# Perceiver block on one core: ScalarE takes the square roots of the first norms, GpSimd loads the small parameters, and some steps of the expert routing change places

## The reference

```python
x = x + xattn(layernorm(x), ctx_1024, ...)   # [c, c2q, c*c2q, c*q2c] @ W_l.T + b_l
x = x + attn(layernorm(x), ...)              # attention, conv of width 3, attention with the new q, out_w
h = layernorm(x)
probs = softmax(h @ gate_w.T); top2_p, top2_i = top_k(probs, 2)
hh = gelu(einsum('nd,edf->nef', h, w1) + b1)
all_out = einsum('nef,efd->ned', hh, w2) + b2
x = x + clip(h + w0 * all_out[n, i0] + w1 * all_out[n, i1], -100, 100)
```

## Time and profile before

| | us |
|---|---|
| median of 3 runs | 432.95 (432.45 to 433.37) |
| the profiled execution, its own time | 431.55 |
| its span, first to last instruction | 429.9 |
| TensorE busy | 409.6 (95%) |
| VectorE busy | 332.9 (77%) |
| ScalarE busy | 212.9 (50%) |
| GpSimd busy | 60.3 (14%) |

### The profile page before, as it was taken

How to read it: one execution, slowest core, us unless ns; L and a number is a source line. 1 busy time by engine, 2 the same in 40 slices (tenths; PEclk the granted TensorE clock), 3 DMA queues, 4 the chain that set the end, 5 groups by cost and what they waited for, 6 DMA issues and landing times.

```text
span 429.9 us, 8272 instructions
## 1 busy us (share of the span) xinstructions
PE 409.6 (95%) x3090; PEld 312.9 (73%) x3090; DVE 332.9 (77%) x618; ACT 212.9 (50%) x369; POOL 60.3 (14%) x80
## 2 busy tenths in 40 slices
PE   1999999999999999999999989999999999999995
PEld 1566565688898899995568745788777778777783
DVE  4758788866259883448977999898998899899666
ACT  4345325130556343131536233796877888778510
POOL 2130000000422120112103701000000000000162
PEclk9999999999999999999999999999999999999998
DMA  7999799999960460009324659889999999995662
GB/s 254 392 379 369 237 401 375 353 408 408 409 236 23 103 247 2 2 3 367 124 93 159 235 208 381 297 324 369 383 387 350 375 382 360 392 368 198 222 193 98
DMA packets 50734, 116.74 MB, mean 272 GB/s; under 512 B 3286, under 2 KB 3302, under 8 KB 50704
## 3 DMA queue, kind: packets, MB, share of 16 engines
q1 hardware_dynamic: 38176, 92.28, 58.3%
q10 hardware_dynamic: 10448, 19.15, 11.6%
q0 software_dynamic: 2080, 4.90, 3.5%
HBM read 94.04 MB, written 21.23 MB: 268 GB/s over the span
## 4 chain that ended last, share of the span: by engine, by line
PE 67%; DMA 13%; DVE 9%; POOL 3%; ACT 3%; issue 3%; SPq 1%; ACTq 0%; DVEq 0%; POOLq 0%
PE banks L2015 4%; PE banks L2013 4%; PE banks L2014 4%; PE banks L2046 4%; DMA w<-in_wlT 3%; PE banks L1734 3%; PE banks L2057 3%; PE banks L2056 3%; PE banks L1623 3%; PE banks L2055 3%; DMA A<-in_ctxT 3%; PE banks L1744 3%; PE banks L1739 3%; PE banks L1624 3%; PE banks L1858 3%
## 5 line engine op out<-in xcount | busy, mean ns | idle before, releaser
L1374 DVE TENSOR_TENSOR w_lo<-w,w_hi 128x1024 fp32r<-128x1024 f32 x48 | 55.5, 1218 | 0.0
L662 ACT ACTIVATE w_hi<-w 128x1024 fp32r<-128x1024 f32 x48 | 47.4, 1094 | 2.1 <-DMA w<-in_w 2.1
L747 ACT ACTIVATE A<-banks,b_sb 128x128 f32<-128x128 f32 x112 | 30.4, 382 | 24.3 <-PE banks L2026 9.3
L2013 PE MATMUL banks<-w_hi,cT_r 128*128 128x512 f32 x100 | 40.1, 401 | 0.0
L2015 PE MATMUL banks<-w_hi,cT_r 128*128 128x512 f32 x100 | 39.0, 390 | 0.0
L2014 PE MATMUL banks<-w_lo,cT_r 128*128 128x512 f32 x100 | 39.0, 390 | 0.0
L858 POOL TENSOR_TENSOR A<-A,hrec 128x1024 f32<-128x1024 f32 x8 | 16.4, 2048 | 66.6 <-DVE hrec L1192 66.6
L900 POOL DMA_DIRECT2D b_sb<-in_b1T x12 | 6.5, 542 | 137.1 <-ACT A L747 121.8
L1623 PE MATMUL banks<-w_lo,A2r 128*128 128x512 f32 x52 | 22.7, 437 | 1.6 <-ACT A2r L529 1.3
L1183 DVE TENSOR_REDUCE hmax<-banks 128x16 f32<-128x1024 f32 x8 | 9.8, 1221 | 18.2 <-PE banks L1809 18.2
L2015 PEld LDWEIGHTS banks<-w_hi,cT_r 128*128 128x128 f32 x100 | 18.8, 188 | 4.0
(11 more groups left out here) (353 smaller groups left out, 1045.0 us busy)
## 6 DMA issues: line engine op xcount, KB each, us to landing
w<-in_w SPq DMA_DIRECT2D x24, 2048.0 KB, 10.3
rows_dram<-A ACTq DMA_DIRECT2D x1, 14592.0 KB, 45.6
A<-in_ctxT SPq DMA_DIRECT2D x8, 1024.0 KB, 11.0
A<-in_ctx SPq DMA_DIRECT2D x8, 1024.0 KB, 9.5
w<-in_w SPq DMA_DIRECT2D x5, 1024.0 KB, 7.6
w<-in_wlT SPq DMA_DIRECT2D x3, 1024.0 KB, 15.0
wqkv<-in_wqkvT SPq DMA_DIRECT2D x1, 3072.0 KB, 16.2
w<-in_convT SPq DMA_DIRECT2D x1, 3072.0 KB, 18.1
```

The costliest lines, as they stand in the source:

```text
L662: nc.scalar.activation(w1_hi[:, u, k * F:(k + 1) * F], w1[:, u, k * F:(k + 1) * F], ACT.Copy).then_inc(hi_ready, 1)
L747: ins = nc.scalar.activation(hT[:, u, f, :], HT[f // 4][:, tile(f % 4)], ACT.Gelu, bias=b1_sb[:, u, f:f + 1])
L1374: nc.vector.tensor_tensor(w1_lo[:, u, part], w1[:, u, part], w1_hi[:, u, part].bitcast(F32), ALU.subtract).then_inc(lo_ready, 1)
L2013: mm(HP[u][c][:, :], xr[:, 0, u, k, :], high[:, at], start=(i == 0), stop=False)
```

## The change

Four things are changed.

1. The beginning. The roots of the four variances are taken by ScalarE (`first_roots`, `other_roots`) instead of Newton steps on VectorE; a first Sqrt on `eps` brings the table in early, and an Exp behind the second brings back the table for the scores. ScalarE rounds both first halves of W_l, then takes the first high part straight from PSUM (`high_first`) and copies `cT` after it.
2. The six small parameters are loaded by GpSimd's queue: `wcq` and `wq` ahead of its first memset, `wc` and the three scalars behind its constants.
3. The routing. VectorE does `place(0)` before `finish(3)` instead of after `norm_by_root(3)`. On TensorE `turn_gate(1)` goes behind `outputs(7)` and now waits for `take_out(7)`; the first half of `out_project(3)` goes ahead of `gate_logits(1)`; `gate_logits(3)` goes ahead of `counts(2)`. `outputs(7)` no longer waits for the copy of the second turned tile.
4. The experts. ScalarE makes the gelu of block 1 before it waits for the store of block 0, and in `output(0)` TensorE turns block 2's rows after seven steps of f instead of four. The scratch `bm`, `bv` of `list_blocks` moves to other columns.

```diff
@@ scalar: beginning
-            for dst, src in ((wcq, "wcqT"), (wq, "wqT")):
-                act.dma_start(dst[:, :], t[src]).then_inc(widths_in, 16)
-            act.dma_start(wc[:, :], t["wcT"]).then_inc(score_params_in, 16)
-            for i, name in enumerate(("b_cq", "b_c", "b_q")):
-                act.dma_start(scal[:, i:i + 1], t[name].to_broadcast([P, 1])).then_inc(score_params_in, 16)
+            first_roots()
             high_wl(0)
+            high_wl(1)
+            high_first()
             copy_cT(0, 0)
-            high_part(0, 0)
-            high_wl(1)
             widen_first()
+            other_roots()
@@ scalar: first experts
+            gelu(1, 1, 16, True)
             store_first(0, 0)
-            gelu(1, 1, 16, True)
@@ gpsimd
+            for dst, src in ((wcq, "wcqT"), (wq, "wqT")):
+                pool.dma_start(dst[:, :], t[src]).then_inc(widths_in, 16)
...
+            pool.dma_start(wc[:, :], t["wcT"]).then_inc(score_params_in, 16)
+            for i, name in enumerate(("b_cq", "b_c", "b_q")):
+                pool.dma_start(scal[:, i:i + 1], t[name].to_broadcast([P, 1])).then_inc(score_params_in, 16)
@@ vector: beginning
-            dve.wait_ge(x_in[0], 16)
-            norm(0)
+            variance_first()
+            dve.wait_ge(root_ready, 1)
+            link(nc.vector.reciprocal(rstd[:, 0:1], sd[:, 0:1]))
+            normalise(0)
...
             low_wl(0)
+            low_wl(1)
+            dve.wait_ge(cT_ready, 1)
             low_part(0, 0)
-            low_wl(1)
-            norm_others()
+            variance_others()
+            dve.wait_ge(root_ready, 2)
+            link(nc.vector.reciprocal(rstd[:, 1:NT], sd[:, 1:NT]))
@@ vector: routing
             norm_by_root(2)
             after_choice(1)
+            place(0)
             finish(3)
             variance(3)
             take_counts(1)
             norm_by_root(3)
-            place(0)
@@ tensor: outputs, turn_gate
                 if m >= 2 * NT - 2:
-                    pe.wait_ge(cT_ready, m + 3)
+                    pe.wait_ge(cT_ready, 2 * NT + 1)
...
-                pe.wait_ge(o_ready, 2 * (NT + min(n + 2, NT)))
+                pe.wait_ge(o_ready, 2 * (NT + min(2 * n + 2, NT)))
@@ tensor: routing
             values(7)
-            turn_gate(1)
             counts(0)
             outputs(7)
+            turn_gate(1)
+            out_project(3, 0)
             gate_logits(1)
-            out_project(3, 0)
             out_project(3, 1)
@@
             dispatch(0, 1)
+            gate_logits(3)
             counts(2)
-            gate_logits(3)
@@ tensor: output
-                        if between and f == FT // 2:
+                        if between and f == FT - 1:
                             between()
```

More of the change, by code:

```diff
@@ L210, in perceiver_kernel @@
         slots_c = A2[:, 4096:4096 + 2 * (NT - 1) * E].rearrange("p (c t e) -> p c t e", c=2, t=NT - 1)
-        bm, bv = (A2[:, at:at + OVER * E * MORE].rearrange("p (o i) -> p o i", o=OVER) for at in (4096, 4608))
+        bm, bv = (A2[:, at:at + OVER * E * MORE].rearrange("p (o i) -> p o i", o=OVER) for at in (6144, 6656))
         cnt = c2q[:, 3 * P:3 * P + NT * 2 * E].rearrange("p (t e) -> p t e", t=NT)
@@ L515, in high_wl, with high_first, first_roots, other_roots @@
                 nc.scalar.activation(wl_hi[:, wl_half(i), :], wl[:, wl_half(i), :], ACT.Copy).then_inc(wl_high, 1)
+            def high_first():
+                act.wait_ge(cT_psum, 1)
+                nc.scalar.activation(pieces(0, 0)[:, 0], turn_bank(0, 0)[:, :].rearrange("p (k n) -> p k n", k=KT),
+                                     ACT.Copy).then_inc(part_high[0], 1)
+            def first_roots():
+                act.wait_ge(var_ready, 1)
+                nc.scalar.activation(steps[:, 0:1], eps[:, 0:1], ACT.Sqrt)
+                act.wait_ge(var_ready, 2)
+                nc.scalar.activation(sd[:, 0:1], mv[:, 0, 1:2], ACT.Sqrt, bias=eps[:, 0:1]).then_inc(root_ready, 1)
+            def other_roots():
+                act.wait_ge(var_ready, 3)
+                nc.scalar.activation(sd[:, 1:NT], mv[:, 1:NT, 1], ACT.Sqrt, bias=eps[:, 0:1]).then_inc(root_ready, 1)
+                nc.scalar.activation(steps[:, 1:2], eps[:, 0:1], ACT.Exp)
             def high_part(part, n):
@@ L709, in root @@
             def root(n):
-                act.wait_ge(var_ready, n)
+                act.wait_ge(var_ready, 3 + n)
                 nc.scalar.activation(sd[:, n:n + 1], mv[:, n, 1:2], ACT.Sqrt, bias=eps[:, 0:1]) \
@@ L932, in norm_by_root @@
             def norm_by_root(n):
-                dve.wait_ge(root_ready, n)
+                dve.wait_ge(root_ready, 2 + n)
                 link(nc.vector.reciprocal(rstd[:, n:n + 1], sd[:, n:n + 1]))
@@ L956, in norm, with variance_first, variance_others @@
                                         ALU.subtract, ALU.mult).then_inc(normed, 1)
-            def norm_others():
-                rest = slice(1, NT)
-                var, r, h = mv[:, rest, 1], rstd[:, rest], sd[:, rest]
+            def variance_first():
+                nc.vector.memset(eps[:, :], EPS).then_inc(var_ready, 1)
+                dve.wait_ge(x_in[0], 16)
+                link(nc.vector.bn_stats(st[:, 0, :], x_res[:, 0, :]))
+                nc.vector.bn_aggr(mv[:, 0, :], st[:, 0, :]).then_inc(var_ready, 1)
+            def variance_others():
                 for n in range(1, NT):
@@ L965, in norm_others @@
                     link(nc.vector.bn_stats(st[:, n, :], x_res[:, n, :]))
[L966 to L975, removed]
+                    ins = nc.vector.bn_aggr(mv[:, n, :], st[:, n, :])
+                    if n < NT - 1:
+                        link(ins)
+                ins.then_inc(var_ready, 1)
             def normalise(n):
@@ L1170, in _ @@
             link(nc.vector.memset(zero_bf[:, :], 0.0))
-            link(nc.vector.memset(eps[:, :], EPS))
             low_c(NT - 2)
```

## The result

| | before | after |
|---|---|---|
| median of the executions (us) | 432.55 (20 runs) | 435.49 (20 runs) |
| ratio of the times | | 1.0075, 95% interval 1.0059 to 1.0090 |
| span of the profiled execution | 429.9 | 433.1 |

One of the 20 executions before took 468.87 us and is left out of the ratio. By the ratio the change costs 3.2 us (2.6 to 3.9); the two medians differ by 2.9. Forecast was +1.45, with +2.65 as the upper end of the range. The direction was right, the size wrong. The median itself, 435.49, lies just inside the recorded range of 432.3 to 435.6, but only because that range was laid around a median of three executions (432.95), which twenty put at 432.55.

What follows compares the result with a forecast made beforehand. TensorE bounds the long stretches; elsewhere a start transfer, routing hand-offs and two tied VectorE and TensorE chains. -0.5 + 1.65 + 0.3 = +1.45 us on 431.55 gives 433.0, plus 1.40 to the median 434.4; range 432.3 to 435.6.

Steps and rivals of the forecast that it cites:

- the start: Up to the first scores: `scores(0)` at about 15.0 instead of 15.56, -0.5 us, between 0 and -0.75.
- the routing: From tile 1's logits to VectorE's take of block 0's rows: +1.65 us, between +0.7 and +2.2.
- Between the ends I go by the packets: Start: packet counts put the small transfers nearer to cheap in GpSimd's queue, so `ctxT` lands 0.8 us earlier.
- the start gives nothing: Rival, chance 0.15: small transfers cost the same in GpSimd's queue, `ctxT` lands at 15.4; 434.9 us.
- the filled hole: Start, TensorE: the 0.33 us wait for the third pair of weights goes; last product ends near 14.8, not 15.2.
- the turning: Routing: `turn_gate(1)` behind `outputs(7)` makes tile 1's logits 2.9 us later; +1.15 us after VectorE's slack.
- the swap: Routing: `gate_logits(3)` ahead of `counts(2)` delays VectorE's taking of the counts by another 0.5 us.
- If a step or two run side by side: Routing: the condition for the lower bound of +0.7 us instead of +1.65.
- Net +0.3 us: First expert blocks: VectorE's gapless chain 0.35 to 0.4 later, TensorE sooner but waiting; between -0.1 and +0.5.
- Smaller routing loss: Rival, chance 0.26: overlap cuts the routing to +0.7, start gives -0.7; sum +0.3, 433.3 us.
- First scores at half clock: Rival, chance 0.05: TensorE's clock is not up at the first scores, their 3.67 us double; 438 us.
- Faster: Rival, chance 0.13: VectorE's chain in the first experts is not the limit, removed TensorE waits gain; -1.15, 431.8 us.

Runs made afterwards that it cites:

- e_start: Kernel before with the new beginning alone (roots, order of high parts, small transfers by GpSimd); 432.43 us against 432.62, ratio 0.9997.
- e_roots: Kernel before with the new beginning, the six small transfers left in ScalarE's queue; 431.81 us against 432.00, ratio 0.9990.
- e_routing: Kernel before with all the routing steps of the change alone; 434.58 us against 432.62, ratio 1.0052.
- x_fill: Changed kernel with 32 small matmuls in TensorE's wait behind `turn_hidden(2)`; 434.71 us against 432.62 for the kernel before, ratio 1.0046.
- e_experts: Kernel before with the experts' edits alone (early gelu, block 2's rows turned at step 7, scratch moved); 433.21 us against 432.62, ratio 1.0017.
- b_lists: Kernel before with early gelu, block 2's rows turned at step 7, `find_last` and `last_places` behind the loop; 428.71 us against 432.00, ratio 0.9927.
- r_turn: Kernel before with the routing steps except `gate_logits(3)` ahead of `counts(2)`; 434.91 us against 432.18, ratio 1.0067.
- e_fill: Kernel before with 12 small matmuls in TensorE's wait ahead of `outputs(7)` in the routing; 431.72 us against 432.18, ratio 0.9990.
- x_roots: Changed kernel with the six small transfers back in ScalarE's queue; ratio 1.0074 to the kernel before.

## Why the prediction was wrong

Term by term in the profiled pair, against the forecast: the start +0.22 (forecast -0.5), the routing +1.79 (+1.65), the first experts +0.36 and the clock +1.61 (together +0.3), the tail -0.8 (no term). Two steps failed, the start's and, with the larger part, that of the first experts.

**The start (-0.5).** "Between the ends I go by the packets": moving the transfers was held to be nearer to cheap, with 0.8 us won on `ctxT`. The packets did fall away from ScalarE's queue, but the stream ran at 268 GB/s instead of 260 from 8 to 12 us, where above 300 was forecast, and `ctxT` landed 0.65 us later. Measured: +0.22 us in the profiled execution, and by the time of e_start -0.1 (-0.9 to +0.7), which excludes neither. The mechanism of the rival "the start gives nothing" is what the traces bear out; its 434.9 would have been the nearer forecast. (Of VectorE's small instructions ahead of the first norm nine went, not eight; the norm was written 1.45 us earlier, 1.5 forecast.) The step on TensorE, the filled hole, was right where the second half of W_l lands in time (e_roots) and moot where it doesn't (2.62 us of waiting in the changed kernel, with landing put at 8.1 and found at 8.8).

**The routing (+1.65).** Right in mechanism, terms and size: 1.3 for the turning (1.15 forecast), 0.5 for the swap (0.5), 1.8 in the trace. A small step was off: the 0.25 us that `counts(0)` was to give VectorE didn't come (`take_out(7)` ends at 217.00, not 216.75), and the logits come at 220.32 instead of 220.0. By the time e_routing costs 2.2 (1.4 to 3.0), which holds 1.8. "If a step or two run side by side" did not happen.

**The first experts (+0.3).** The VectorE part was right (0.36), and so was the wait that TensorE gets in exchange. The step "Net +0.3 us" failed: a wait off the critical path was priced at nothing, and this one took the granted clock from 1.00 to 0.5 for the 3.3 us behind it, 1.61 us in the profile. x_fill shows it: with work in the wait the clock stays at 1.00 and the 1.61 us are gone from the profile. By the times all of the experts' edits cost +0.7 (0.0 to 1.5); why that is less than the 2.0 of the profile is open, as told at e_experts.

**The ground of the sum.** The shift from the profiled execution to the median (1.40 us) was taken as a constant. Against twenty executions it is 1.00, and it is hardly one: the executions of the kernel before stand around 431.8 and 433.2 us, and a sum from one profile doesn't say how many executions an edit moves from one group to the other. With what was measured the sum is 0 or 0.2 + 1.8 + 0.4, and the clock, tail and noise for the other 0.8 to 1.0 of the 3.2.

**The rivals.** "Smaller routing loss" fell with e_routing. "First scores at half clock" did not come (the scores take 3.79 us, not twice 3.67), though the half clock lasted longer at the start and cost TensorE its readiness. "Faster" was wrong for this change and right about the waits, as b_lists shows.

## What to carry to other kernels

A wait on the busiest engine that nobody needs can still cost: ask what the clock does behind it, and fill it, split it, or take the slack out of the other engine. When two chains tie, undoing waits on one of them is worth nothing or less; look for what can leave the other chain altogether, as the 3.6 us of small instructions here that were needed only some 140 us later. And before summing against one profiled execution, see how the executions spread and why: here the executions stood in two groups, and the profile was of one of them.

## What the runs showed of the hardware

- Behind TensorE waits of 2.67 to 2.82 us the granted clock fell in 4 of 4 profiles, behind waits of 1.78 to 2.17 us in 1 of 9 (2.08 us, in r_turn). A fall lasts 3 to 4 us at 0.50 and costs 1.3 to 1.7 us where TensorE sets the pace; in r_turn, behind 253 us, where VectorE does, 0.9.
- The clock also falls in the routing without a long wait (0.2 and 0.8 us, short matmuls between them): in 3 of 10 profiles with that order of instructions.
- 32 small matmuls in a wait of 2.7 us kept the clock at 1.00 (x_fill). 12 in a wait of 0.8 us: undecided (e_fill).
- With the six small transfers in either queue the stream at the start has a dent: from 10 to 11 us it ran at 112 and 130 GB/s with them in GpSimd's queue (the changed kernel, e_start), at 123, 166 and 203 in ScalarE's (e_roots, before, x_roots). That they cause it isn't shown.
- The start of the first scores, which waits for a 1 MB transfer, differs by some 0.8 us between executions of the same beginning (15.27 to 16.07 with the old one).
